# A decoder layer on one core: each batch's output projection is issued in the next batch's attention turn

## What is computed

```python
x = _layernorm(x + _L0_attn_ref(x, w_q, w_k, w_v, w_out), axis=-1)
x = _layernorm(x + _L0_xattn_ref(x, ctx_4096, xattn_weight), axis=-1)
x = _layernorm(x + _L0_ffn_ref(x, w_gate, w_up, w_down), axis=-1)
# in _L0_ffn_ref:
scale = jnp.clip(jnp.mean(jnp.abs(w)), EPS)
wq = jnp.clip(jnp.round(w / scale), -1.0, 1.0) * scale
```

## Time and profile before

| | us |
|---|---|
| median of 3 runs (1495.33 to 1499.22) | 1496.32 |
| the profiled execution, its own time | 1498.48 |
| span in its trace | 1496.7 |
| PE busy | 1385.3 |
| DVE busy | 1123.8 |

### The profile page before, as it was taken

The page is one execution under the profiler, slowest core; times in us unless marked ns, Lnnn a source line. Parts: engine busy times, 40 slices in busy tenths (PEclk is TensorE's granted clock), DMA queues, the critical chain, the costliest instruction groups (busy, mean ns, idle before and its releaser), DMA issues.

```text
span 1496.7 us, 23086 instructions
## 1 busy us (share of the span) xinstructions
PE 1385.3 (93%) x7576; PEld 693.7 (46%) x7576; DVE 1123.8 (75%) x1895; ACT 539.1 (36%) x1107; POOL 247.2 (17%) x270
## 2 busy tenths in 40 slices
PE   6787999999999999999999978999999999999996
PEld 2343555555445444444444544444444444444443
DVE  2885564456398788788888847888888888888884
ACT  4764644565423223313313323223223222222221
POOL 1122122212131221321321412000000000000000
PEclk9898999999999999999999988999999999999999
DMA  9413544454434434434334249222222222222200
GB/s 368 196 33 96 195 152 153 133 189 153 153 100 142 159 99 148 152 104 165 130 120 150 78 122 282 71 71 70 81 84 82 76 70 84 70 70 70 70 14 29
DMA packets 63571, 178.92 MB, mean 120 GB/s; under 512 B 15360, under 2 KB 26672, under 8 KB 63536
## 3 DMA queue, kind: packets, MB, share of 16 engines
q1 hardware_dynamic: 63536, 178.48, 36.7%
HBM read 153.02 MB, written 25.43 MB: 119 GB/s over the span
## 4 chain that ended last, share of the span: by engine, by line
issue 48%; PE 21%; DVE 12%; POOL 7%; DMA 5%; ACT 3%; SPq 2%; DVEq 0%; POOLq 0%; ACTq 0%
PE ps L479 18%; DMA ctx<-ctx 5%; DVE below L1019 2%; PE ps L470 2%; POOL simw L1327 2%; PE ps L571 1%; POOL q L1302 1%; DVE weights L999 1%; ACT prob L733 1%; DVE rope_s L856 1%; POOL k L1280 1%; ACT tern L805 1%; PE ps L553 1%; DVE dot L1099 1%; POOL rstd L1297 1%
## 5 line engine op out<-in xcount | busy, mean ns | idle before, releaser
L479 PE MATMUL ps<-weights,xT 128*128 128x512 f16 x2160 | 483.3, 380 | 7.5 <-DVE weights L1118 6.3
L479 PEld LDWEIGHTS ps<-weights,xT 128*128 128x128 f16 x2160 | 208.4, 98 | 251.7 <-issue 7.8
L624 PE MATMUL ps<-weights 128*128 128x512 fp8e4 (+1 forms) x1536 | 300.0, 357 | 0.9 <-issue 0.9
L624 PEld LDWEIGHTS ps<-weights 128*128 128x128 bf16 x1536 | 146.8, 98 | 155.9 <-issue 1.4
L479 PE MATMUL ps<-weights 128*128 128x512 f16 x768 | 172.2, 385 | 7.1 <-issue 5.7
L650 PE MATMUL ps<-weights 128*128 128x512 fp8e4 x704 | 157.4, 380 | 0.0
L825 ACT ACTIVATE weights<-ps,xscale 128x512 f32<-128x512 f32 x96 | 61.7, 643 | 251.4 <-PE ps L624 251.4
L733 ACT ACTIVATE prob<-prob,negmax,undo 128x128 f32<-128x128 f32 x256 | 122.7, 483 | 34.6 <-DVE negmax L1038 34.6
L479 PEld LDWEIGHTS ps<-weights 128*128 128x128 f16 x768 | 75.3, 99 | 101.7 <-issue 13.8
L667 ACT COPY qkT<-ps 128x512 f32<-128x512 f32 x64 | 34.4, 589 | 205.3 <-PE ps L470 205.3
L1297 POOL TENSOR_TENSOR rstd<-rstd,expo 128x1 f32<-128x1 f32 x32 | 17.4, 542 | 536.0 <-DVE rstd L928 536.0
(11 more groups left out here) (142 smaller groups left out, 1811.1 us busy)
## 6 DMA issues: line engine op xcount, KB each, us to landing
wch<-w_ffn SPq DMA_DIRECT2D x96, 688.0 KB, 4.2
wch<-sim_scratch SPq DMA_DIRECT2D x96, 128.0 KB
ternary_scratch<-tern SPq DMA_DIRECT2D x48, 172.0 KB, 1.9
ctx<-ctx SPq DMA_DIRECT2D x16, 512.0 KB
weights<-x SPq DMA_DIRECT2D x16, 512.0 KB, 10.2
x_scratch<-weights SPq DMA_DIRECT2D x16, 512.0 KB, 2.9
weights<-x_scratch SPq DMA_DIRECT2D x16, 512.0 KB, 3.3
out<-k SPq DMA_DIRECT2D x16, 512.0 KB, 2.6
```

What stands on the lines that cost most here:

```text
L479: ins = nc.tensor.matmul(ps[:, bank], partsT[:, a, t], weights[:, t, w, half * HALF:(half + 1) * HALF], start=(t == 0 and a + w == 0), sto ...
L624: ins = nc.tensor.matmul(ps[:, 2 * w + a, 0:n], xqT[:, t], w8m[:, t, at:at + n], start=(t == 0), stop=(t == KT - 1))
```

## The change

On PE the output projection of batch b leaves the end of turn b. Its two products stand in turn b + 1, ahead of `scores(0)` and ahead of `scores(1)`, and `proj(0)` to `proj(5)` move back by as many places. Turn 15 does those of batches 14 and 15. DVE's turn is written as three lists (first, rest, last), in each of which the residual and the first norm are those of the batch before. POOL's `rstd` of the first norm moves to the next turn's start, SP's store of the normed residual to between two chunks of the next turn, SP's load of the residual to the turn's end. ACT's `high_x` stands at the turn's start, and `abs_chunk` and `ctx_square` in other places; at the start the squares of a matrix are no longer interrupted. `x1p` takes the place of `wo_raw`, `weigh(0, kk)` moves into turn 15, and each matrix's norm has a PSUM bank of its own. No work is added but a copy of one factor (`undo_out`).

```diff
@@ sync: turn
+                def store_x1(n):
+                    sp.wait_ge(x1_ready, n + 1)
+                    sp.dma_start(x1_dram[...], xres).then_inc(x1_stored, 16)
                 if mode != "plain":
                     for c in range(2, SUMS if mode == "sum" else CUTS):
+                        if c == 4 and not first:
+                            store_x1(b - 1)
                         if mode == "cut":
                             w_store(c - 2)
                         w_load(c)
...
                 sp.wait_ge(sims_ready, b + 1)
...
-                sp.wait_ge(x1_ready, b + 1)
-                sp.dma_start(x1_dram[...], xres).then_inc(x1_stored, 16)
+                if has_next:
+                    residual_load()
@@ tensor: turn
                 qk_T(0)
-                proj(0)
+                if first:
+                    proj(0)
+                else:
+                    pe.wait_ge(w_split, 4 * KT)
+                    out_proj(b - 1, 0)
                 scores(0)
                 qk_T(1)
-                proj(1)
+                if first:
+                    proj(1)
+                else:
+                    out_proj(b - 1, 1)
                 scores(1)
+                if not first:
+                    proj(0)
                 prob_T(0)
-                proj(2)
-                pv(0)
+                proj(2 if first else 1)
...
+                pv(0)
-                proj(3)
+                proj(3 if first else 2)
...
@@ scalar: turn and start
                 for w in range(2):
                     copy_bank(w, tr_pair(b, 0), qkT[:, w])
+                if has_next and not first:
+                    high_x(b + 1)
+                if not first:
+                    abs_chunk(0)
                 act.wait_ge(scores_full, b * 2 + 1)
                 for w in range(2):
                     copy_bank(w, tr_pair(b, 1), qkT[:, w])
                 exps(0)
...
+                abs_chunk(6)
                 if has_next:
                     v_chunk(b + 1, 0)
-                if has_next2:
-                    high_x(b + 2)
+                abs_chunk(7)
                 if has_next:
                     v_chunk(b + 1, 1)
-                abs_chunk(6)
-                abs_chunk(7)
...
             for n in range(KT):
                 square(n)
-                if n == 1:
-                    high_x(1)
+            high_x(1)
+            for n in range(KT, 2 * KT):
+                square(n)
@@ vector: turn
+                def turn_rest():
+                    low_x(b + 1)
+                    cut_chunk(0)
+                    residual_half(b - 1, 0)
+                    mask_max(0)
+                    cut_chunk(1)
+                    normalise(0)
+                    first_norm(b - 1, residual_half(b - 1, 1))
+                    cut_chunk(2)
+                    rope(b + 1, 0)
+                    mask_max(1)
+                    rope(b + 1, 1)
+                    normalise(1)
+                    ctx_norms()
+                    oT_low_part(0)
+                    cut_chunk(3)
+                    rope(b + 1, 2)
+                    if has_next2:
+                        x_maximum(b + 2)
+                    cut_chunk(4)
+                    rope(b + 1, 3)
                     oT_low_part(1)
+                    ctx_dots()
+                    if has_next2:
+                        x_factors(b + 2)
+                        x_undo(2)
+                    cut_chunk(5)
+                    next_undo()
```

More of the change, by code:

```diff
@@ L1068, in turn @@
-                split_more(2, 7, 8)
-                mask_max(1)
-                if last:
-                    conv_low_part(0, 2)
-                dve.wait_ge(ctx_squared, b + 1)
-                dve.wait_ge(sims_ready, b)
-                nc.vector.reduce_sum(nsq[:], sq[:], AX_X).then_inc(norms_ready, 1)
-                cut_chunk(0)
-                normalise(1)
-                if has_next:
-                    rope(b + 1, 2)
-                oT_low_part(0)
-                if last:
-                    residual(0, 0)
-                    norm_sums(x2n)
@@ L1083, in turn, with residual_half @@
-                cut_chunk(1)
-                if has_next:
-                    rope(b + 1, 3)
-                if first:
+                def residual_half(n, c):
+                    dve.wait_ge(xres_loaded, n * 16 + 16)
+                    dve.wait_ge(pj_full[c], pj_out(n) + 1)
+                    half = xres[:, c * HALF:(c + 1) * HALF]
+                    nc.vector.scalar_tensor_tensor(out=half, in0=ps[:, PJ + c], scalar=undo_out[:, 0:1], in1=half,
+                                                   op0=ALU.mult, op1=ALU.add).then_inc(pj_free[c], 1)
+                    dve.wait_ge(pj_free[c], pj_out(n) + 1)
+                    return st.done(nc.vector.bn_stats(stats[:, c], half))
@@ new lines, in first_norm @@
+                def first_norm(n, s):
+                    st.wait(s)
+                    apart(dve)
+                    s = st.done(nc.vector.bn_aggr(mv[:], stats[:].rearrange("p a b -> p (a b)")))
+                    st.wait(s)
+                    nc.vector.tensor_scalar(rstd[:, 0:1], mv[:, 1:2], EPS_LN, None, ALU.add).then_inc(var_ready, 1)
+                    dve.wait_ge(rstd_ready, n + 1)
+                    nc.vector.tensor_scalar(xres, xres, mv[:, 0:1], rstd[:, 1:2], ALU.subtract, ALU.mult) \
+                        .then_inc(x1_ready, 1)
@@ L1090, in turn @@
                     st.wait(st.done(nc.vector.tensor_tensor(undo[:, 0, 1:2], xfit[:, 7:8], wboth[:, 1:2], ALU.mult)))
-                if has_next2:
-                    x_maximum(b + 2)
-                split_more(3, 0, 4)
-                cut_chunk(2)
-                if last:
+                    x_maximum(2)
+                    split_w(3, range(4))
+                    ctx_dots()
+                    oT_low_part(1)
+                    split_w(3, range(4, KT))
+                    x_factors(2)
@@ L1112, in turn @@
-                dve.wait_ge(xres_loaded, b * 16 + 16)
-                for c in range(2):
-                    if c == 1 and not has_next:
-                        xqT_out(0)
-                    dve.wait_ge(pj_full[c], pj_out(b) + 1)
-                    half = xres[:, c * HALF:(c + 1) * HALF]
-                    nc.vector.scalar_tensor_tensor(out=half, in0=ps[:, PJ + c], scalar=undo[:, 0, 1:2], in1=half,
-                                                   op0=ALU.mult, op1=ALU.add).then_inc(pj_free[c], 1)
-                    dve.wait_ge(pj_free[c], pj_out(b) + 1)
-                    s = st.done(nc.vector.bn_stats(stats[:, c], half))
-                    if c == 0:
-                        cut_chunk(5)
-                    if c == 0 and has_next and not has_next2:
+                    ctx_norms()
@@ L1304, in turn, with first_rstd @@
             def turn(b, mode, has_next, has_next2):
+                first = isinstance(b, int) and b == 0
+                def first_rstd(n):
+                    pool.wait_ge(var_ready, n + 1)
+                    nc.gpsimd.tensor_tensor(rstd[:, 1:2], rstd[:, 0:1], expo[:, 0, 0:1], ALU.pow).then_inc(rstd_ready, 1)
+                if not has_next:
+                    pool.wait_ge(conv_max_all, 1)
+                    for w in range(2):
+                        pool.wait_ge(pj_full[w], pj_uses(B - 1, 5) + 1)
+                    nc.gpsimd.memset(down8[64:P, IT - 1], 0.0).then_inc(padded, 1)
+                    pool.wait_ge(padded, 1)
+                if not first:
+                    first_rstd(b - 1)
+                if not has_next:
+                    rstd_out(1)
                 if has_next:
@@ L1307, in turn @@
                     rope_add(b + 1, 1)
+                    if first:
+                        rope_add(b + 1, 2)
                 pool.wait_ge(ctx_loaded, b * 32 + 32)
@@ L1310, in turn @@
                 nc.gpsimd.tensor_tensor(sq[:, 0:8], ctx9[:, 0:8], ctx9[:, 1:9], ALU.mult).then_inc(ctx_mult, 1)
-                if not has_next:
-                    rstd_out(1)
-                if has_next:
+                if has_next and not first:
                     rope_add(b + 1, 2)
-                if isinstance(b, int) and b == 0:
+                if first:
+                    rope_add(b + 1, 3)
                     w_root(3)
@@ L1336, in turn @@
                 if has_next and not has_next2:
-                    pool.wait_ge(sims_ready, b + 1)
-                    for w in range(2):
-                        pool.wait_ge(pj_full[w], pj_uses(B - 1, 5) + 1)
-                    st.wait(st.done(nc.gpsimd.memset(down8[64:P, IT - 1], 0.0)))
                     nc.gpsimd.memset(x1p[:, 0:1], 0.0).then_inc(set_up2, 1)
```

210 lines of the change are left out of this document (123 added, 87 removed).

## The result

The changed kernel takes 1562.5 us (1559.7 to 1565.9, four runs) against 1496.1 in the same session: 1.044 times as long, 95% interval 1.041 to 1.047. The profiled execution has a span of 1562.8 us, at a granted clock of 0.954.

A forecast was written before the change was run, and what follows sets the result against it. PE bound turns of sums, PE and DVE both filled turns of cuts; the change closes a loop of 35.5 + 20.0 + 7.8 = 63.3 us. Phase 2 moves from 926.6 to 991.3, +64.7 on 1498.5: 1563, stated as 1560, range 1535 to 1592.

The forecast's parts named there:

- the loop: Turns of cuts: each first cut waits through DVE, POOL and SP for the one before, 63.3 us against 54.55.
- Leg 1: DVE, from the start of cut_chunk(0) to the end of x_maximum: 35.5 us.
- leg 2: POOL, from the end of x_maximum to the last cosines, with the all-reduce between: 20.0 us.
- leg 3: SP, from the cosines through their stores and the residual's load to the landing of w_load(0): 7.8 us.
- Rival (b): POOL shows one gap instead of two around the all-reduce: turns of cuts 56.1 us, total about 1505; chance 0.07.
- (c): POOL's part and the load's landing take longer, PE's half clock counts: 67 us a turn, about 1590; chance 0.08.
- Turns of sums: Turns 2 to 5: the loop runs over ACT's abs_chunk(0), 51.8 us a turn, over PE's 49.68.
- The start: Up to scores(1) of turn 1: waits for squares go, output projection starts at 130.8; scores(1) at 145.8, gain 0.3 us.
- Turns 13 to 15: Turn 13 ends at 890.3; turn 14 takes 49.7 + 7.1 us, the residual being late; turn 15 takes 44.2.
- The room: Turns of cuts: DVE and PE both full, a better order could bring 54.55 us to about 50.5.
- rival (a): The loop is short and the new order works: turns of cuts 50.5 us, total about 1458; chance 0.10.

The follow-up runs named there:

- Run 4: Kernel before, with only DVE's cut_chunk(0) moved to the head of the turn: 1527.3 us, ratio 1.021.
- run 1: Changed kernel, with the next turn's first two chunk loads issued ahead of SP's wait for the cosines: 1542.8 us.
- run 2: Changed kernel, with POOL making the cosines ahead of the all-reduce and DVE's ctx_dots ahead of x_maximum: 1533.8 us.
- run 3: Changed kernel, with a plain POOL copy instead of the all-reduce of x's maximum from batch 2 on: 1488.5 us.
- run 5: Changed kernel, with the residual's load and the next turn's first two chunk loads ahead of SP's wait for the cosines: 1482.2 us.
- run 7: Changed kernel, with the residual's load alone moved ahead of SP's wait for the cosines: 1545.4 us.
- run 8: Changed kernel with early residual and chunk loads, and SP's wait for the cosines and their stores moved into the next turn: 1468.3 us.

## Why the prediction was right, point by point

**The time.** 1560 was predicted, 1562.5 measured, with the loop as the reason. Run 4 closes the same loop in the kernel before, runs 1 to 3, 5, 7 and 8 shorten or cut it in the changed one, and where a loop still binds, the turn is the sum of its legs. That the number is as near as 2.5 us is in part luck: turns 6 to 13 came out 5.1 us shorter from first cut to first cut, what stood before them 2.6 longer and turn 15 3.3 longer.

**The legs.** Leg 1 was put at 35.5 and measured 35.9; leg 2 at 20.0, measured 18.6; leg 3 at 7.8, measured 7.9. The errors partly cancel: 63.3 against 62.6. Leg 2 was read from turn 3, whose gaps around the all-reduce were long (7.1 and 7.8 us); in the changed kernel they were 6.1 and 6.7, near those of turn 10. The cosines, once POOL had come to them, took 3.4 us, as in turn 3, and not the 6 of turn 10. POOL waited for DVE's dots in none of these turns. It was its own instructions that took less, as the first of these rows (turn 10 before) and the second (turn 10 after) show; DVE stood still in the second, as the prediction had said, and whether that is the cause was not tested.

```profile
665.00 2.70 POOL L1327 TENSOR_TENSOR simw<-simw,expo 128x9 f32<-128x9 f32 x1
```

```profile
706.92 1.85 POOL L1429 TENSOR_TENSOR simw<-simw,expo 128x9 f32<-128x9 f32 x1
```

Turn 10's gaps and turn 3's cosines together would have given 18.6.

**POOL.** Rival (b), one gap around the all-reduce, is out, and so are the longer legs of (c). The all-reduce ended 6.5 us after the maximum, and 6.70 of "issue" followed it. The Trainium skill (GPSIMD Engine Reference, Instruction dispatch) gives about 6 us of code loading for the first call to a freshly loaded kernel; each gap in this trace is of about that size, 6.1 and 6.7 us, and there are two per all-reduce. What fills them the trace does not show.

**Turns of sums.** 51.8 was predicted (its pieces add up to 51.9); the rows above give 51.6. Turn 3 took 53.6, and the first cut of turn 6 came at 404.8 instead of 402.2. The start was put at a gain of 0.3 and was a loss of 1.5: `scores(1)` of turn 1 at 147.6, not 145.8. PE's first projection gained 6.1, not 7.5. The step that was off is the time when PE could start the output projection, 133.8 and not 130.8. ACT was done with chunk 4 at 126.7, not 124.5, and from there to the start of chunk 6, at 131.8, it was 5.1 us and not the 4.3 of before.

**Turns 13 to 15.** Turn 13 ended at 888.5 (890.3 predicted). Turn 14 took 56.8, exactly as summed, with 5.2 of wait for the residual's mask (5.4) and `scores(1)` at half clock. Turn 15 took 47.5, not 44.2: the added products filled less of PE's idle time than I thought. Phase 2 began at 992.8 (991.3).

**The room.** I had written that a better order could bring a turn of cuts to about 50.5. Run 8 reached 51.2. What I had as rival (a), the new order without its loop, was therefore real. It needed three more moves on SP, and came to 1468 instead of 1458: its turns of cuts were 0.7 us longer than I had put them, some 5 in all, and turn 6 kept its wait for the thresholds.

**What I had missed.** The prediction named the chunk's load as the loop's last leg, and the residual only in turn 14. Three more loops run through the wait for the cosines: the residual's gave a turn of 59.7 (run 1), that over `w_store(5)` 60.4 (run 2), the third chunk's 53.8 (run 5). The prediction's number did not hang on them, since the longest loop sets the time, but the expectations of runs 1, 2 and 5 did, and each missed its range.

## What to carry to other kernels

When work moves to the head of a loop's body, follow what it waits for back through every in-order queue to the body before; if the path ends at the work itself, add up its legs and compare the sum with the time of a turn. A queue that waits for a late result closes such a loop for everything issued behind it, so count all of it: taking out one of two gave 20 us, taking out both 80. When an experiment misses its number, read its rows before you drop the theory. A control in the kernel before is worth its run, since it can find a gain that has nothing to do with the change.

## What the runs showed of the hardware

In turns 7 to 13 of the changed kernel each all-reduce on POOL ended 6.5 to 6.8 us after its operand was there, 0.4 of it work, and the next `rope_add` began 6.7 to 7.8 us behind it: some 13 to 14 us around 0.4 of work. With a copy in its place (run 3) that `rope_add` began as soon as its operand was there. The same POOL instruction on 128 x 9 elements took 2.70 us in one turn and 1.85 in others. Behind a wait of 10.3 us PE's sixteen matmuls of `scores(1)` took 2.08 us, behind one of 5.2 us too, and behind waits of 2 us 1.16; the granted clock was 0.50 in the 3 us in which such a block of 2.08 ran in turn 15 of the kernel before, the lower of the two levels. Over the turns of cuts it was 0.92, and 1.00 with the waits gone in run 8.
